# Decoder layer: keys and values in one product, and the rotary rotation by row copies

## The reference

```python
x = x + attention(layernorm(x))            # 16 query heads, 2 key/value heads, 32 wide, causal
x = x + mamba(ctx, z=layernorm(x))         # selective scan over 512 steps, 16 states, gated by silu(z)
x = x + ffn(layernorm(x))                  # gated FFN, 1408 wide, with the two best of 8 low-rank adapters
```

```python
q = (x @ wq.T + bq).reshape(b, l, 16, 32)
k = (x @ wk.T + bk).reshape(b, l, 2, 32)
v = (x @ wv.T + bv).reshape(b, l, 2, 32)
# rotary position: per head, x1 the first 16 columns, x2 the last 16
rope(x) = concat([x1 * cos - x2 * sin, x2 * cos + x1 * sin])
q, k = rope(q), rope(k)
```

## Time and profile before

| | us |
|---|---|
| median of 3 runs | 1518.23 |
| lowest and highest run | 1510.87, 1524.10 |
| the profiled execution | 1524.03 |
| its span, first to last instruction | 1522.2 |

### The profile page before, as it was taken

One profiled execution on the slowest core, in us unless ns is written; L12 is line 12 of the kernel. 1 busy time (PEld: TensorE's weight loads), 2 busy tenths in 40 slices (PEclk: granted clock), 3 DMA queues, 4 the chain that ended last, 5 costly groups with the idle time before them and its releaser, 6 DMA issues.

```text
span 1522.2 us, 15997 instructions
## 1 busy us (share of the span) xinstructions
PE 1368.4 (90%) x5768; PEld 673.0 (44%) x5768; DVE 1021.4 (67%) x1203; ACT 701.7 (46%) x1490; POOL 89.6 (6%) x116
## 2 busy tenths in 40 slices
PE   6747777999999899899999799899999799799999
PEld 2324444444444465444444365444444355444443
DVE  4799996578989645669898744748988944511110
ACT  5445653365542385365552276455553177211110
POOL 0000001000000000000000000100000000100000
PEclk8955569999999699999999689999999879699999
DMA  5376661147767600127766700126766620011202
GB/s 200 70 191 147 137 141 31 41 121 176 187 151 170 152 2 2 44 72 183 186 162 156 188 11 2 42 64 151 188 162 159 154 67 2 0 31 52 62 31 83
DMA packets 53277, 158.80 MB, mean 104 GB/s; under 512 B 5072, under 2 KB 10704, under 8 KB 44752
## 3 DMA queue, kind: packets, MB, share of 16 engines
q0 software_dynamic: 9216, 67.11, 22.1%
q1 hardware_dynamic: 25664, 54.23, 10.8%
q10 hardware_dynamic: 18320, 36.45, 8.5%
HBM read 86.20 MB, written 4.46 MB: 60 GB/s over the span
## 4 chain that ended last, share of the span: by engine, by line
PE 66%; DVE 21%; ACT 6%; issue 4%; DMA 3%; ACTq 0%; DVEq 0%; POOL 0%
PE ps_a L858 21%; PE ps_a L870 9%; DVE state L1040 8%; PE ps_a L938 5%; PE ps_b L878 5%; PE ps_a L784 5%; PE ps_w L837 4%; PE ps_b L798 3%; DVE state L1035 3%; PE ps_w L746 3%; DMA y_sb<-state 3%; DVE state L1045 3%; PE ps_w L904 2%; ACT r L590 2%; DVE neg_max L1075 2%
## 5 line engine op out<-in xcount | busy, mean ns | idle before, releaser
L858 PE MATMUL ps_a<-xt,w_sb 128*128 128x512 f32 x704 | 320.0, 609 | 6.4 <-DVE r L1211 6.4
L1040 DVE TENSOR_TENSOR_SCAN state<-decay,state 128x2048 f32<-128x2048 f32 x64 | 282.7, 4417 | 2.1
L1211 DVE TENSOR_TENSOR r<-r,ps_a 128x512 f32<-128x512 f32 x132 | 90.2, 685 | 189.3 <-ACT r L642 189.3
L858 PEld LDWEIGHTS ps_a<-xt,w_sb 128*128 128x128 f32 x704 | 137.0, 196 | 180.8 <-issue 180.8
L642 ACT ACTIVATE r<-ps_a 128x512 f32<-128x512 f32 x132 | 78.4, 596 | 268.2 <-PE ps_a L858 122.7
L590 ACT ACTIVATE r<-ps_a,neg_max 128x128 f32<-128x128 f32 (+3 forms) x256 | 134.1, 539 | 121.4 <-DVE neg_max L1075 116.0
L784 PE MATMUL ps_a<-r 32*128 32x512 f32 (+3 forms) x512 | 137.0, 620 | 51.6 <-ACT r L590 34.2
L548 ACT ACTIVATE decay<-dt_sb,decay_rate 128x511 f32<-128x511 f32 x256 | 163.2, 710 | 18.3 <-DVE state L1040 17.9
L870 PE MATMUL ps_a<-r,wb_sb 128*128 128x512 f32 x352 | 166.2, 595 | 4.5 <-DVE r L1211 2.2
L938 PE MATMUL ps_a<-wd_sb,r 128*128 128x512 f32 x352 | 163.3, 616 | 0.0
L1035 DVE TENSOR_TENSOR state<-du_sb,bc_sb 128x2048 f32<-128x2048 f32 x64 | 146.1, 2283 | 9.0 <-DMA bc_sb<-bc_rows 5.2
(11 more groups left out here) (117 smaller groups left out, 1392.9 us busy)
## 6 DMA issues: line engine op xcount, KB each, us to landing
y_sb<-state POOLq DMA_DIRECT2D x64, 1024.0 KB, 9.5
bc_sb<-bc_rows ACTq DMA_DIRECT2D x64, 512.0 KB, 5.4
w_sb<-in_w_tiles SPq DMA_DIRECT2D x44, 512.0 KB, 8.0
wd_sb<-in_w_down SPq DMA_DIRECT2D x44, 256.0 KB, 3.2
wb_sb<-in_w_adapt SPq DMA_DIRECT2D x44, 128.0 KB, 2.1
xa<-in_x SPq DMA_DIRECT2D x4, 1024.0 KB, 5.2
out_x<-xb SPq DMA_DIRECT2D x16, 256.0 KB, 8.1
xn_att<-in_ctx_t SPq DMA_DIRECT2D x4, 512.0 KB, 7.8
```

The costliest lines, as they stand in the source:

```text
L858: mm = nc.tensor.matmul(ps_a[:, 2 * (f % 2) + half, :], w_sb[:, slot, at + k * P:at + (k + 1) * P], xt[:, k, :], start=(k == 0), stop=Fals ...
L1040: nc.vector.tensor_tensor_scan(flat, decay[:, n % 2, :, :].rearrange("p j l -> p (j l)"), flat, 0.0, ALU.mult, ALU.add).then_inc(scan_chai ...
```

## The change

Keys and values become one 128-row tile, tile 0, made by one projection: rows are key head 0, value head 0, key head 1, value head 1. PE transposes this tile in slot 3 (`VALUES_AT`), and DVE picks the value columns out of it in slot 4 with four small copies. The rotated keys are copied by two 32-row DMAs over the value rows (`copy_keys`, slot 8), which gives the doubled keys. The rotation is no longer a product on PE: SP waits for ACT's copy of a tile and issues eight DMAs of 16 rows from `q_raw` to `q_rot`, which swap the halves; the sign goes into the table of sines; DVE multiplies `q_rot` by it. The permutation matrix, the separate value weights, and the products, copies and transposes that used them go. Queries are now tiles 1 to 4. For batch 0 the rotations stand in SP's stream behind the first loads; for the others each stands behind a load of down weights.

```diff
+VALUES_AT = 3
+COPY_AT = 8
 def projections(f):
     raw = f - 1 if 1 <= f <= TILES else None
-    back = f - 2 if 2 <= f <= TILES + 1 else None
-    return raw, back, {TILES + 2: 0, TILES + 3: 1}.get(f)
+    turned = f - 2 if 2 <= f <= TILES + 1 else None
+    return raw, turned
...
-            raw, back, _ = projections(f)
-            names += [("raw", raw)] * (raw is not None) + [("back", back)] * (back is not None)
+            raw = projections(f)[0]
+            names += [("raw", raw)] * (raw is not None) + [("vt", 0)] * (f == VALUES_AT)
...
+        q_rot = r2[:, 6:8, :]
...
+            def rotate(b, n):
+                bank, count = use(("raw", n), b)
+                sp.wait_ge(work_free[bank], count + 1)
+                for p in range(0, P, HD):
+                    for to, of in ((p, p + HD // 2), (p + HD // 2, p)):
+                        sp.dma_start(q_rot[to:to + HD // 2, n % 2, :], q_raw[of:of + HD // 2, n % 2, :])\
+                            .then_inc(rot_loaded[n % 2], 16)
+            def copy_keys(b):
+                sp.wait_ge(qk_ready, b * TILES + 1)
+                for p in (0, 2 * HD):
+                    sp.dma_start(k_t[p + HD:p + 2 * HD, :], k_t[p:p + HD, :]).then_inc(k_copied, 16)
+            def beside_down(b, f):
+                if 0 <= f - 3 < TILES:
+                    rotate(b, f - 3)
+                if f == COPY_AT:
+                    copy_keys(b)
...
                 for f in range(FT):
                     load_wd(t, f)
+                    if t + 1 < BATCH:
+                        beside_down(t + 1, f)
...
+            for n in range(TILES):
+                rotate(0, n)
+            copy_keys(0)
...
+                    if n == 2:
+                        of, turned = use(("vt", 0), b)
+                        act.wait_ge(work_full[of], turned + 1)
-                    bias = q_bias[:, n:n + 1] if n < MT else vec[:, V_BQ + n:V_BQ + n + 1]
+                    bias = q_bias[:, n - 1:n] if n > 0 else vec[:, V_BKV:V_BKV + 1]
...
-                if projections(f)[2] == 0:
-                    act.wait_ge(v_full, b + 1)
-                    act.wait_ge(qk_ready, b * TILES + TILES)
-                    nc.scalar.activation(q_raw[:, 0, :], ps_b[:, 0, :], ACT.Identity,
-                                         bias=vec[:, V_BV:V_BV + 1]).then_inc(v_moved, 1)
...
-                        w = wq_sb[:, k, raw * P:(raw + 1) * P] if raw < MT else wk_sb[:, k, :]
+                        w = wq_sb[:, k, (raw - 1) * P:raw * P] if raw > 0 else wkv_sb[:, k, :]
...
-                if back is not None:
-                    bank = fill(pe, ("back", back), b)
-                    raw_bank, raw_count = use(("raw", back), b)
+                if f == VALUES_AT:
+                    raw_bank, raw_count = use(("raw", 0), b)
                     pe.wait_ge(work_free[raw_bank], raw_count + 1)
-                    nc.tensor.matmul(ps_w[:, bank, :], rot, q_raw[:, back % 2, :], start=True, stop=True)\
-                        .then_inc(work_full[bank], 1)
-                if values == 0:
...
+                    bank = fill(pe, ("vt", 0), b)
                     for i in range(NT):
-                        mm = nc.tensor.transpose(ps_b[:, 0, i * P:(i + 1) * P], q_raw[:, 0, i * P:(i + 1) * P], ident)
-                    mm.then_inc(v_turned, 1)
+                        mm = nc.tensor.transpose(ps_w[:, bank, i * P:(i + 1) * P], q_raw[:, 0, i * P:(i + 1) * P], ident)
+                    mm.then_inc(work_full[bank], 1)
...
                 pe.wait_ge(qk_ready, (b + 1) * TILES)
-                pe.wait_ge(v_ready, b + 1)
+                pe.wait_ge(k_copied, 32 * (b + 1))
+                pe.wait_ge(v_ready, NT * (b + 1))
...
                     tt(rope_tmp, q_raw[:, n % 2, :], cos_t, ALU.mult).then_inc(rope_chain, 1)
-                    bank = filled(dve, ("back", n), b)
-                    part = q_t[:, n, :] if n < MT else k_t
-                    tt(part, ps_w[:, bank, :], sin_t, ALU.mult).then_inc(work_free[bank], 1)
+                    of_parity = (TILES + 1 - n % 2) // 2
+                    dve.wait_ge(rot_loaded[n % 2], 16 * 2 * (P // HD) * (b * of_parity + n // 2 + 1))
+                    part = q_t[:, n - 1, :] if n > 0 else k_t
+                    tt(part, q_rot[:, n % 2, :], sin_t, ALU.mult).then_inc(rope_chain, 1)
...
-                    nc.vector.tensor_copy(v_sb[:], ps_b[:, 0, :].rearrange("p (i d) -> p i d", i=NT)[:, :, 0:VD])\
-                        .then_inc(v_ready, 1)
+                if f == VALUES_AT + 1:
+                    bank = filled(dve, ("vt", 0), b)
+                    turned = ps_w[:, bank, :].rearrange("p (i g c d) -> p i g c d", i=NT, g=KV_HEADS, c=2)
+                    for i in range(NT):
+                        copied = nc.vector.tensor_copy(v_sb[:, i, :].rearrange("p (g d) -> p g d", g=KV_HEADS),
+                                                       turned[:, i, :, 1, :])
+                        copied.then_inc(v_ready, 1)
+                    dve.wait_ge(v_ready, NT * (b + 1))
+                    nc.vector.tensor_copy(scrap[:], ps_w[0:1, bank, 0:1]).then_inc(work_free[bank], 1)
...
-    c[:, C_SIN:C_SIN + L] = np.sin(ang)
+    c[:, C_SIN:C_SIN + L] = np.where(p % HD < half, -1.0, 1.0).astype(np.float32)[:, None] * np.sin(ang)
```

More of the change, by code:

```diff
@@ L35 @@
 BG, BU, WADAPT = 0, P, 2 * P
[L37 to L42, removed]
+C_ID, C_MASK, C_COS, C_SIN = 0, 128, 256, 768
+C_CAND, C_HALF = 1280, 1288
+C_COLS = 1292
+V_CW, V_CB, V_DTB, V_AL, V_D, V_BQ, V_BKV = 0, 16, 20, 24, 88, 92, 96
+V_COLS = V_BKV + 1
 VD = KV_HEADS * HD
@@ L279, in decoder_layer @@
         qk_ready = sem("qk_ready")
-        v_full = sem("v_full")
-        v_moved = sem("v_moved")
-        v_turned = sem("v_turned")
+        rot_loaded = [sem(f"rot_loaded{k}") for k in range(2)]
+        k_copied = sem("k_copied")
         v_ready = sem("v_ready")
@@ L738, in project @@
             def project(b, f):
-                raw, back, values = projections(f)
+                raw = projections(f)[0]
                 if raw is not None:
@@ L1047, in rotate @@
             def rotate(b, f):
-                total = TILES
-                _, n, values = projections(f)
+                n = projections(f)[1]
                 if n is not None:
@@ L1054, in rotate @@
                     tt(rope_tmp, q_raw[:, n % 2, :], cos_t, ALU.mult).then_inc(rope_chain, 1)
[L1055 to L1067 removed]
+                    of_parity = (TILES + 1 - n % 2) // 2
+                    dve.wait_ge(rot_loaded[n % 2], 16 * 2 * (P // HD) * (b * of_parity + n // 2 + 1))
+                    part = q_t[:, n - 1, :] if n > 0 else k_t
+                    tt(part, q_rot[:, n % 2, :], sin_t, ALU.mult).then_inc(rope_chain, 1)
+                    dve.wait_ge(rope_chain, 2 * (b * TILES + n + 1))
+                    tt(part, part, rope_tmp, ALU.add).then_inc(qk_ready, 1)
+                    dve.wait_ge(qk_ready, b * TILES + n + 1)
+                if f == VALUES_AT + 1:
[7 more added lines that the diff above has]
+                    nc.vector.tensor_copy(scrap[:], ps_w[0:1, bank, 0:1]).then_inc(work_free[bank], 1)
             def attention(b, slots):
@@ L1280, in constant_table @@
     half = HD // 2
-    for m in range(P):
-        if m % HD < half:
-            c[m + half, C_ROT + m] = -1.0
-        else:
-            c[m - half, C_ROT + m] = 1.0
     c[:, C_MASK:C_MASK + P] = np.where(p[None, :] <= p[:, None], 0.0, NEG)
-    for k in range(32, P):
-        c[k, C_SEL + k % 32] = 1.0
     inv = (np.float32(10000.0) ** (-np.arange(half, dtype=np.float32) / np.float32(half))).astype(np.float32)
@@ L1312, with keys_values @@
     heads = np.concatenate([np.arange(h * HD, (h + 1) * HD) for m in range(MT) for h in tile_heads(m)])
-    kv_rows = np.repeat(np.arange(KV_HEADS * HD).reshape(KV_HEADS, HD), HPT // KV_HEADS, axis=0).reshape(-1)
+    def keys_values(k, v):
+        return np.concatenate([part[g * HD:(g + 1) * HD] for g in range(KV_HEADS) for part in (k, v)])
     xw = a["L0_xattn_x_proj_w"].T
@@ L1336 @@
         column(a["L0_xattn_D"]), column(a["L0_attn_bq"][heads]),
-        a["L0_attn_bk"][kv_rows][:, None],
-        np.tile(a["L0_attn_bv"], P // VD)[:, None],
+        keys_values(a["L0_attn_bk"], a["L0_attn_bv"])[:, None],
     ], axis=1)
@@ L1343 @@
         "wq": rows(a["L0_attn_wq"][heads].T),
-        "wk": rows(a["L0_attn_wk"][kv_rows].T),
-        "wv": rows(np.tile(a["L0_attn_wv"].T, (1, P // VD))),
+        "wkv": rows(keys_values(a["L0_attn_wk"], a["L0_attn_wv"]).T),
         "wo": rows(a["L0_attn_wo"][:, heads].T),
```

27 lines of the change are left out of this document (5 added, 22 removed).

## The result

The change makes the kernel slower: 1549.89 us, median of four runs (1549.16 to 1552.99), beside 1520.89 us for four runs of the kernel before (the three that stand ahead of the prediction, and 1523.56). The ratio is 1.0206, 95% interval 1.0154 to 1.0258. The profiled execution took 1549.62 us, span 1548.0 (before 1524.03 and 1522.2). The forecast was 1524 us, in a range of 1506 to 1540: the time lies outside it.

The account below looks back on a forecast made before the run. DVE and the state transfer were taken to bound the down stage's second half. Late copies cost 3.6 us in batches 1 to 3 and 2.0 in batch 0, 5.6 us on the 1518.23 median: 1524 us, range 1506 to 1540.

Parts of the forecast that it names:

- The reading of the bound: Down stage, batch 1: PE leads to about 457 us, then DVE and the state transfer; PE time saved behind that gains nothing.
- The prize: Down stages: DVE's sine product no longer waits for PE's rotation product, 15.3 us in all, about 1.0% of the time.
- rival B: Copies slip between the state transfer's packets and land free: 10 us won, 1508 us; chance 0.20.
- DVE's work for the values: Down stage: four small value copies and a one-element read on DVE, net loss 0.8 us per batch.
- E: Fast-side rival: PE is the bound after all, its 7.8 us come back in batches 1 to 3: 23 us, 1495; chance 0.04.
- 0.37 us apart: SP's queue: spacing of two ready loads taken for the copies, so a tile's last copy is issued 2.6 us after ACT's copy.
- nothing at tiles 1, 2 and 4: Down stages: next to no waits for the copies at these tiles, which land before or while DVE works on earlier pieces.
- The landing: Tiles 0 and 3: copies land like 256 KB loads beside the state transfer, 5.3 and 7.8 us after issue.
- Rival C: Short packets need more turns: 9.9 us from last issue to landing at tiles 0 and 3, 31 us lost, 1549; chance 0.12.
- Rival D: Eight copies of a tile served one after the other, 15.2 us a tile, at least 124 us lost, 1642; chance 0.04.
- PE's idle time: Ahead of attention: PE idle some 13 us or more instead of 5.54; clock already at its lower level, so no cost.
- The first half of the change: Keys and values by one product, keys doubled by DMA, values copied by DVE, rotation still on PE; cost 0.8 us a batch.

Follow-up runs that it names:

- merge_late: Kernel before with keys and values by one product, rotation still on PE, and two gate and up weight tiles asked for after attention's third scan; 1521.55 us, ratio 1.0023.
- ruler: Kernel before plus five bursts of eight copies on SP's queue in the last batch's FFN, one shape a burst, to price an issue; 1520.16 us.
- no_copy: Changed kernel without the rotation's copies and without DVE's wait for them, their place set to zero once; 1510.02 us, ratio 0.9946.
- one128: Changed kernel with one plain 128-row copy a tile in place of the eight 16-row copies, halves not swapped; 1527.11 us, ratio 1.0064.
- thin: Changed kernel with the same eight copies a tile, each of 64 columns in place of 512; 1549.81 us, ratio 1.0216.
- after_late: Whole change with one wait moved: the first two gate and up weight tiles asked for after attention's third scan; 1546.35 us, ratio 1.0188.
- back_first: Kernel before with PE doing the last tile's rotation product ahead of the next projection; 1507.45 us, ratio 0.9937.

## Why the prediction was wrong

**What held.** The reading of the bound: DVE ends last in the second half of the stage, and PE's saving is no gain there. The waits for PE are gone, as foretold. The prize was on the path: free copies give 1510 us, near rival B's 1508, and moving the product gives 1507. DVE's work for the values, 0.8 us a batch, was right in size: the four copies take 0.62 us and the read 0.14. That it lengthens a batch by as much is not borne out (merge_late). E is out: what PE saved did not come back, and the stage is 5 to 11 us longer.

**The step that failed: the issue, "0.37 us apart".** The earlier trace rows gave the time from the first issue of a pair to the second. The second load itself took 0.43 us in that row, so a burst goes at 0.47 us, which the ruler confirms for loads from DRAM; and both rows are loads from DRAM, where the change copies from SBUF, at 0.63 us. Beside the state transfer a single issue took up to 2.15 us. So the last of eight copies went out 4.3 to 9.1 us after the first, and not 2.6. I had bounded the landing from both sides, but not the issue; it had one row, taken as if it were the operation itself.

**The step that fell with it: nothing at tiles 1, 2 and 4.** With 2.6 us of issue a tile the queue is idle between tiles, and each tile stands by itself. At 5 to 10 us a tile it is nearly always busy: in batch 1, SP issues from 445 to 486 us with pauses of 0.8 and 2.2 us ahead of tiles 2 and 3. A late tile then hands its delay to the next, and the down weights queue with them. In batch 2, tiles 0, 1, 3 and 4 all wait, 1 and 4 because their last copies, so late, land beside the next state's traffic.

**The landing: placed at the wrong tiles.** It was put at that of a 256 KB load beside the transfer, 5.3 and 7.8 us, behind the last issue at tiles 0 and 3. There the last copy lands after 1.9 to 3.5 us in the change; the landings of 6.0 to 6.4 us are at tiles put at nothing. By itself, with one copy a tile, the landing at tiles 0 and 3 beside a transfer is 8.1 to 9.9 us, longer than those rows say, and by the step from no_copy to one128 it costs 18 us.

**Rival C gave 1549 us, and the time was 1549.9: luck, since C's mechanism was not what happened.** It laid 9.9 us on the landing behind the last issue at tiles 0 and 3, where 1.9 to 3.5 was measured. Rival D had the shape: copies one after the other. It placed them in the DMA engines at 1.9 us each, and they are in series in SP's queue, at some 0.6 to 2.15 us, while their landings overlap: batch 0's first tile, with no state transfer beside it, had landed 6.4 us after its first issue, where eight in series make 15.2. D was to decide from 8 us a tile; 8 of the 20 tiles took that for the issue alone, and the time stayed far below its 1642. The rule that I weighed for D, from the Trainium skill, page "DMA: Bandwidth & Descriptors", section "Rules for kernel authors", holds in its advice: one transfer in place of eight was worth 21.6 us here. The estimate of 16.6 us a tile does not. Its fixed cost of about 2.0 us, which the page fits to transfers issued by GpSimd, is near the 1.9 us that a free copy took here; but the copies overlap, and the tiles took 6.3 to 12.3 us from the first issue to the last landing.

**A step that came out either way: PE's idle time.** It was to grow to 13 us ahead of attention. In the profiled execution of the change it shrank to 1.12 us from 5.54, and to 0.73 and 0.56 in the later batches, because the down weights arrive late and PE's last products move to the end of the stage. Eight copies do not force this: in thin and after_late, which have as many, it grew to between 6.7 and 11.2 us. PE's timeline, two lines of the change and one of after_late:

```profile
507.87 5.79 PE L948 MATMUL ps_a<-wd_sb,r 128*128 128x512 f32 x8 [5.15 <-DMA wd_sb<-in_w_down]
...
518.21 0.49 PE L794 MATMUL ps_a<-r 32*128 32x128 f32 x4 [1.12 <-DVE xb L1237]
```

```profile
519.60 0.80 PE L794 MATMUL ps_a<-r 32*128 32x128 f32 x4 [8.22 <-DVE xb L1237]
```

**The first half of the change** was costed at the value copies alone. Its larger price, 6.5 us by merge_late, is an indirect one: attention starts earlier and thereby asks earlier for weights, ahead of a transfer that DVE needs. I had named the queues of the stage, but not what the start of attention triggers.

## What to carry to other kernels

Count DMA instructions as work on the queue that issues them: a burst of k copies costs k times the issue, measured on the same kind of source and beside the same traffic, before the first byte of the last one moves. Where a bound is drawn, draw it for the issue as for the landing. Read the landing of the copy that is waited for, the last of a burst: a median over all copies told nothing of it here. And where one engine waits for another's product, look first at the order of the two products on that engine: here it gave, for one moved block, what the DMA was to bring.

## What the hardware showed that I had not expected

In a burst of eight, an issue on SP's queue costs 0.63 to 0.68 us for a copy out of SBUF and 0.46 to 0.47 for a load out of DRAM, with 16 rows or 128 (ruler). Beside a running accumulating transfer of 1 MB, issued by POOL, many issues of SP and ACT stretch to between 1 and 2.3 us; with a quarter of that transfer 6 of SP's 160 are left. What in the hardware they share was not tried and stays open.

A copy of 32 KB that lands in 1.9 to 2.0 us where nothing else runs took 6.0 to 6.4 us when it went out within 0.2 us of a 512 KB broadcast, and a single copy of 256 KB beside the 1 MB transfer landed 0.2 to 0.3 us after that transfer (one128, ten times).

The clock at the start of attention follows what PE did before it. After 5.54 us of idle time the granted clock was 0.50, the lower level, and a first score product took 0.80 us. After 1.12 us of idle time in the change it was 0.83 over the first 5 us and the product took 0.49 us. After 8.22 us in after_late it took 0.80 us again. With the rotation product moved it is the same: 0.49 us in batches 1 and 2, after 1.73 and 0.47 us of idle time, and 0.80 us in batch 3, after 8.21 us; that profiled execution was the fastest of its ten. PE's timeline and the busy times by stretch (columns as above; PEclk is the third number from the end) of back_first:

```profile
498.35 0.49 PE L784 MATMUL ps_a<-r 32*128 32x128 f32 x4 [1.73 <-DVE xb L1224]
```

```profile
498.00:503.00 5.00, 3.79 (x24) 2.08 (x24) 3.06 (x8) 2.69 (x13) 0.17 (x1) 0.82 0.97 223
```
